# The tail of a fused attention and tree feed-forward kernel: other order of the last batch's gathers, one value sum moved to TensorE, one tree moved behind the last gather's issue

## The reference

```python
x = x + xattn(layernorm(x), ctx_1024, ctx_1024, ...)   # 16 heads of 64, 2048 keys
x = x + attn(layernorm(x), ...)                        # 8 heads of 16: xpos, decay mask, group norm, silu gate
x = x + ffn(layernorm(x), ...)
...
def _fff(x, nw, nb, w1, b1, w2, b2, act):              # a tree: 8 levels, 256 leaves
    node = jnp.zeros(x.shape[:2], dtype=jnp.int32)
    for _ in range(DEPTH):
        logit = jnp.einsum('bsd,bsd->bs', x, nw[node]) + nb[node]
        node = 2 * node + 1 + (logit > 0).astype(jnp.int32)
    leaf = node - NN
    h = act(jnp.einsum('bsd,bsdl->bsl', x, w1[leaf]) + b1[leaf])
    return jnp.einsum('bsl,bsld->bsd', h, w2[leaf]) + b2[leaf]
...
    q, k, v = _fff(xn, *q_params, relu), _fff(xn, *k_params, relu), _fff(xn, *v_params, relu)
    att = softmax(einsum('bqd,bkd->bqk', q, k) / sqrt(D))
    y = xn + einsum('bqk,bkd->bqd', att, v)
    return y + _fff(y, *f_params, gelu)
```

## Time and profile before

| | us |
|---|---|
| median of 3 executions | 669.51 |
| lowest, highest | 668.91, 670.25 |
| the profiled execution | 669.95 |
| its span (first to last instruction) | 667.8 |
| PE busy | 622.6 (93% of the span) |
| DVE busy | 452.3 (68%) |
| ACT busy | 394.2 (59%) |
| POOL busy | 275.8 (41%) |

### The profile page before, as it was taken

How to read it: one execution, slowest core, us unless ns; L and a number is a source line. 1 busy time by engine, 2 the same in 40 slices (tenths; PEclk the granted TensorE clock), 3 DMA queues, 4 the chain that set the end, 5 groups by cost and what they waited for, 6 DMA issues and landing times.

```text
span 667.8 us, 10976 instructions
## 1 busy us (share of the span) xinstructions
PE 622.6 (93%) x4225; PEld 536.9 (80%) x4225; DVE 452.3 (68%) x800; ACT 394.2 (59%) x836; POOL 275.8 (41%) x266
## 2 busy tenths in 40 slices
PE   7899999999999999898999999999999998878686
PEld 3688888999998989787988898778989897755564
DVE  2566656778776777777777777786777776853833
ACT  4665556677654555768565854957566755631541
POOL 3210002031110106896252447876161539864832
PEclk9999999999999999999999999999999999998998
DMA  9800000020100008040030037210210044203813
GB/s 197 229 33 1 1 1 0 1 64 32 33 1 1 1 2 306 19 131 0 1 132 1 1 116 276 72 60 1 80 52 1 6 157 168 68 1 128 342 61 130
DMA packets 21402, 48.54 MB, mean 73 GB/s; under 512 B 1508, under 2 KB 14696, under 8 KB 17256
## 3 DMA queue, kind: packets, MB, share of 16 engines
q0 software_dynamic: 4608, 34.74, 13.9%
q1 hardware_dynamic: 16168, 12.85, 7.1%
q10 hardware_dynamic: 576, 0.26, 0.2%
HBM read 47.59 MB, written 0.26 MB: 72 GB/s over the span
## 4 chain that ended last, share of the span: by engine, by line
PE 64%; POOL 13%; DVE 10%; ACT 6%; DMA 4%; issue 2%; SPq 1%; POOLq 0%; DVEq 0%; ACTq 0%
PE ps_s L434 22%; PE ps_av L434 20%; PE ps_ring L664 13%; PE ps_ring L434 4%; POOL leaf L1435 4%; PE ps_m L434 4%; ACT prob L993 2%; POOL leaf L1439 2%; DVE chunk_max L1286 2%; DVE pt_lo L1078 2%; DMA leaf<-up_v_dram,idx 2%; ACT pt_hi L924 2%; DMA leaf<-w_o_dram 2%; POOL ct_lo L1404 1%; DVE hid L1135 1%
## 5 line engine op out<-in xcount | busy, mean ns | idle before, releaser
L924 ACT CAST pt_hi<-ps_ring 128x512 fp32r<-128x512 f32 x256 | 144.5, 590 | 147.8 <-PE ps_ring L664 147.5
L1078 DVE TENSOR_TENSOR pt_lo<-ps_ring,pt_hi 128x512 fp32r<-128x512 f32 x256 | 170.3, 686 | 64.0 <-ACT pt_hi L924 63.9
L993 ACT ACTIVATE prob<-ps_s,neg_max 128x1024 f32<-128x1024 f32 x128 | 141.6, 1113 | 27.2 <-DVE neg_max L1369 27.1
L664 PE MATMUL ps_ring<-ident,prob 128*128 128x128 f32 x1024 | 145.0, 274 | 12.1 <-DVE q_lo L1078 4.9
L1286 DVE TENSOR_REDUCE chunk_max<-ps_s 128x1 f32<-128x1024 f32 x128 | 150.5, 1215 | 5.3 <-PE ps_s L434 5.1
L434 PE MATMUL ps_av<-pt_hi,c_hi 128*128 128x256 f32 x512 | 151.2, 295 | 0.0
L664 PEld LDWEIGHTS ps_ring<-ident,prob 128*128 128x128 f32 x1024 | 116.9, 141 | 39.3 <-issue 18.9
L434 PE MATMUL ps_av<-pt_lo,c_hi 128*128 128x256 f32 x512 | 144.7, 283 | 0.0
L434 PE MATMUL ps_av<-pt_hi,c_lo 128*128 128x256 f32 x512 | 144.7, 283 | 0.0
L434 PE MATMUL ps_s<-ct_hi,q_hi 128*128 128x512 f32 x256 | 112.5, 440 | 3.9 <-ACT prob L993 1.8
L434 PE MATMUL ps_s<-ct_hi,q_lo 128*128 128x512 f32 x256 | 101.4, 396 | 0.0
(11 more groups left out here) (267 smaller groups left out, 765.3 us busy)
## 6 DMA issues: line engine op xcount, KB each, us to landing
stage<-ctx_t_dram SPq DMA_DIRECT2D x16, 256.0 KB, 3.4
stage<-ctx_rows_dram SPq DMA_DIRECT2D x16, 256.0 KB, 2.9
leaf<-w_v_dram SPq DMA_DIRECT2D x1, 512.0 KB, 8.0
leaf<-w_o_dram SPq DMA_DIRECT2D x1, 512.0 KB, 10.2
dec<-decay_dram SPq DMA_DIRECT2D x1, 512.0 KB
nw<-node_w_dram SPq DMA_DIRECT2D x1, 510.0 KB
wsm<-w_small_dram SPq DMA_DIRECT2D x1, 448.0 KB
leaf<-wq_t_dram SPq DMA_DIRECT2D x1, 384.0 KB, 11.6
```

Source lines behind the costliest of these rows:

```text
L664: last = nc.tensor.transpose(o[:, i * P:(i + 1) * P], prob[:, n % 2, k:k + P], ident[:])
L924: nc.scalar.copy(pt_hi[:, pp, row:row + KPC, P * (n % 2):P * (n % 2 + 1)], ps_ring[:, i % 2, :].rearrange("p (k q) -> p k q", k=KPC)).then ...
L993: nc.scalar.activation(prob[:, n % 2, 1024 * e:1024 * (e + 1)], ps_s[:, 1024 * e:1024 * (e + 1)], ACT.Exp, bias=neg_max[:, n:n + 1], accum ...
L1078: return nc.vector.tensor_tensor(o, a, b_, op)
```

## The change

At the start: `w_v` and `w_o` get a semaphore each; `turn0` is issued behind the query product of slot 0 and waits for `w_v` alone, `join0` for `w_o`; ACT copies these products one slot later than before, in the middle of the slot. Third batch: POOL's `fold2` and `out2` go; PE adds the value tree's blocks instead (`value_sum`, 9 products in the place `v_half` and 8 in `v_rest`), ACT copies the sum out; the fillers of 5 and 8 there go; `y`, `y_t`, `logits_f`, `path_f` and their partners move behind the last batch's `score1` and `yv`; `res` moves behind `gate`. Its fourth tree (`hid3`, `gelu`, `down3`, `own3`, `third_sum`, `third_copy`) moves from ahead of the last batch's first trees to behind the last batch's `pick_f`. Last batch: one cast for three indices after all three picks, then gathers as up q, down q, up k, down k, up v, down v; DVE makes all of the first tree's up-product (POOL's 7 blocks go to it); the filler of 38 becomes 3, with 5 more behind the bias product. `y` and `res` of the last batch get their own room.

```diff
 BEFORE_LAST_AT = {
+    ("PE", "qk_t"): 72, ("PE", "att"): 73.5, ("PE", "v_half"): 73, ("PE", "v_rest"): 76, ("PE", "attp_t"): 76, ("PE", "attv"): 77.5, ("PE", "y_t"): 80,
+    ("PE", "logits_f"): 81, ("PE", "path_f"): 82,
+    ("ACT", "qk_t"): 73, ("ACT", "att"): 76, ("ACT", "attp_t"): 77, ("ACT", "v_sum_copy"): 78, ("ACT", "y_t"): 81, ("ACT", "gelu"): 106,
+    ("ACT", "down3"): 107,
+    ("DVE", "attmax"): 75, ("DVE", "y"): 80, ("DVE", "turns_f"): 82, ("DVE", "pick_f"): 83, ("DVE", "hid3"): 107,
+    ("Pool", "res"): 82, ("Pool", "gather3"): 83, ("Pool", "up3"): 1000, ("Pool", "weigh3"): 1000, ("Pool", "fold3"): 1000,
...
-    ("PE", "third_sum"): 90,
+    ("PE", "third_sum"): 107,
...
-    ("ACT", "load_exp"): 93,
-    ("ACT", "third_copy"): 94,
+    ("ACT", "load_exp"): 1000,
+    ("ACT", "third_copy"): 108,
...
-    ("Pool", "fold2"): 74,
-    ("Pool", "out2"): 74,
+    ("Pool", "fold2"): 1000,
+    ("Pool", "out2"): 1000,
...
-WARM = {("att", B - 2): 5, ("attv", B - 2): 8, ("gated_t", B - 1): 11, ("xf_t", B - 1): 12}
-WARM_THIRD, WARM_LAST = 18, 38
+WARM = {("gated_t", B - 1): 11, ("xf_t", B - 1): 12}
+WARM_THIRD, WARM_LAST, WARM_BLOCKS = 18, 3, 5
...
-        return (7, 10, 0) if t < 3 else (8, 8, 4)
+        return ((0, 10, 0), (7, 10, 0), (7, 10, 0), (8, 8, 4))[t]
...
-VALUE_ACT = VALUE_PE | {0: [], 1: ["turn0", "join0", "turn1"]}
+VALUE_ACT = {1: ["turn0"], 2: ["join0", "turn1"], 3: ["join1", "turn2"], 4: ["join2"], 5: ["queries"], 7: ["turn3"], 9: ["join3"]}
...
+            def value_sum(by_pool):
+
+                rows, o = down_rows_at(B - 2, 2), ps_av[:, 2 * P:3 * P]
+                if by_pool:
+                    pe.wait_ge(S["av_taken"], PAIRS)
+                    pe.wait_ge(S["got_down2"], 16 * (B - 1))
+                    mm(o, ident[:], rows[:, W1:DOWN_ROW], True, False)
+                    pe.wait_ge(S["v_weighed"], 1)
+                    for l in range(LW // 2, LW):
+                        mm(o, ident[:], rows[:, D * l:D * (l + 1)], False, False)
+                else:
+                    pe.wait_ge(S["weighed"], 4 * (B - 2) + 3)
+                    for l in range(LW // 2):
+                        last = mm(o, ident[:], rows[:, D * l:D * (l + 1)], False, l == LW // 2 - 1)
+                    last.then_inc(S["v_summed"], 1)
+
...
                     pe.wait_ge(S[f"got_down{t}"], 16 * B)
                     add(rows[:, W1:DOWN_ROW], t < 3)
+                    if t == 3:
+                        warm(WARM_BLOCKS)
                     by_act(0, n // 2)
...
-                        pe.wait_ge(S["ld_wvo"], 32)
+                        pe.wait_ge(S["ld_wv"], 16)
...
+                elif k == "v_sum_copy":
+                    act.wait_ge(S["v_summed"], 1)
+                    nc.scalar.copy(tree[:, 2, :], ps_av[:, 2 * P:3 * P]).then_inc(S["v_out_ready"], 1)
...
+                elif k == "gather_up01" and last:
+                    pool.wait_ge(S["picked"], 4 * b + 3)
+                    nc.gpsimd.tensor_copy(idx[:, 0:3], chosen[:, 0:3]).then_inc(S["idx_ready"], 3)
+                    pool.wait_ge(S["idx_ready"], 4 * b + 3)
+                    pool.wait_ge(S["ring_filled"], RING[("T", HEADS - 1, CH - 1)] + 1)
+                    pool.wait_ge(S["ring_free"], BY_DVE[("X", HEADS + 3, 0)])
+                    for t in range(3):
+                        gather_up(b, t)
+                        gather_down(b, t)
...
                 elif k == "res":
                     pool.wait_ge(S["y_ready"], b + 1)
-                    if last:
-                        pool.wait_ge(S["third_sum"], 1)
-                    nc.gpsimd.tensor_tensor(res[:], y[:], x2[:], ALU.add).then_inc(S["res_ready"], 1)
+                    nc.gpsimd.tensor_tensor(res[b], ys[b], x2[:], ALU.add).then_inc(S["res_ready"], 1)
```

More of the change, by code:

```diff
@@ L1570, in rest @@
                 elif k == "gather_up2":
[L1572 to L1573 removed]
                     if not last:
[L1576 removed]
+                        gather(b, 2)
+                elif k == "gather_down2" and not last:
+                    pool.wait_ge(S["hid_ready"], 4 * b + 2)
                     gather_down(b, 2)
```

79 lines of the change are left out of this document (37 added, 42 removed).

## The result

| | before | changed |
|---|---|---|
| median, first set (20 executions each) | 669.82 us | 671.88 us |
| lowest, highest | 666.60, 674.48 | 669.86, 675.67 |
| ratio of the first set, 95% interval | | 1.0042 (1.0027 to 1.0058) |
| ratio of a second set (6 against 23 executions) | | 1.0073 (1.0045 to 1.0101) |
| profiled execution, its span | 669.95, 667.8 | 671.89, 670.1 |

The change made the kernel slower, by 2 to 5 us (0.4% and 0.7% in the ratios). The time of 671.9 lies above the predicted range (665.4 to 670.6).

The account below looks back on a forecast made before the run. TensorE held 64% of the chain, nearly all in the 64-head pipeline; only its start and the time behind its end could move. Terms -0.45-2.5+0.4+0.1+2.0-1.4 = -1.85 gave 667.7 us, range 665.4 to 670.6.

Parts of the forecast that it names:

- Start: Start of the head pipeline: the third exponential begins when its maximum is ready, -0.45 us, bounds 0 and 0.6.
- Third batch's value sum: Behind the drain: GpSimd's fold leaves the chain for 17 TensorE products, -2.5 us, bounds 1.7 to 3.8.
- The forecast that the clock would fall again in this stretch: Drain to gate: clock low for somewhat over half of the filler of 11, limiting the gain to 2.5 us.
- Gather order: Last batch's gathers: one cast waits for the third pick, up v lands later, +0.4 us, bounds -0.2 and +0.7.
- The 0.9 us that an undisturbed queue was to give back: Last batch's gathers: without GpSimd's slow second cast, up v may land up to 0.9 us earlier.
- The condition that I had written down for a wrong prediction: Block sums: prediction wrong if `sum1` ends more than 1 us later than before, relative to up v's landing.
- Fourth tree taken out of the wait: Wait for the last batch's gathers: removal frees nothing, TensorE starts `sum0` cold, mostly hidden, +0.1 us.
- The same tree behind the last pick: Behind the last pick: GpSimd's cast ends with VectorE's product, delaying both f gathers and all behind, +2.0 us.
- The rival that the cast isn't held up: Last pick: GpSimd's cast escapes the delay, so 2.0 us leaves the sum, 665.7 us; chance 0.13.
- if the delay doesn't come, that cover still holds: Behind the last pick: the rest of the third batch's tree stays hidden even without the cast's 2.0 us delay.
- Last sum: End of the kernel: products leading up to the last sum make it 4.1 us instead of 5.48, -1.4 us.
- The slower one (671.3): Rival: cold TensorE in the block sums behind the gathers or in the last sum, 671.3 us; chance 0.13.

Follow-up runs that it names:

- cast first: Changed kernel with VectorE's product of the third batch's fourth tree waiting for GpSimd's last index cast; 673.05 us, ratio 1.0054 against the kernel before.

## Why the prediction was wrong, step by step

*Start: right and too small to matter* (-0.44 for -0.45). What I had not reckoned with is that the landing of the load ahead of it moves by 2.5 us from run to run, and that a long wait there is followed by a low clock.

*Third batch's value sum: right in kind, somewhat too large.* Taken between traces at the same clock it is -1.84, at the lower end of my bounds (1.7 to 3.8). The -3.76 between the two profiled executions is 1.84 and a fall of the clock in the trace of before that the changed one happened not to have. The forecast that the clock would fall again in this stretch holds for 11 of 14 traces with the sum on TensorE, but not for the changed kernel's profiled one. The mistake in the step: I took a fall of the clock in one trace for a property of the kernel's place when it comes in some executions and not in others. (With the fold the clock fell in one trace of three, so the two other traces of that code are 1.9 us shorter than the one I worked from.)

*Gather order: the step that failed.* I costed the order by the time at which up v lands, +0.4, and that part came out as +1.08 - 0.02: the cast began 0.76 later behind the first pick, where 0.67 was forecast, and there was 0.59 of idle time behind the cast of three columns where it was 0.28 behind one. The 0.9 us that an undisturbed queue was to give back did not come; the 17.4 us from first issue to up v's product stayed 17.4. The real loss was elsewhere, in a stretch that the sum has at +0.1. A moved DMA has to be followed into every queue in which something waits for it. I followed the order to VectorE (the first tree's product and reduction, over 5 us after the first landing, costs nothing: right) and not to GpSimd, where `up1` stands ahead of `weigh0` and waits for up k, now third. That is +2.98 between the two profiled executions, larger than any term of my sum, and with it in place of the +0.1 the forecast 667.7 would have been 670.6. About half of it is the wait itself and half the clock at which the products behind it ran; against both traces of the old code, and up to the last cast, it is 2.1 to 2.8. The condition that I had written down for a wrong prediction, that `sum1` ends over 1 us later relative to up v's landing, is what came (+2.98).

*Fourth tree taken out of the wait: right in that it costs nothing by itself.* TensorE was idle and cold as I wrote: 11.64 us idle ahead of the first product of `sum0`, clock 0.50 up to about 635. The slow spell was longer than the five or six blocks that I took, but with the weights late its price can't be told from that of the wait. The run with fillers shows that warming it ahead of the wait brings nothing as long as the weights are late. With the weights on time the stretch to the copy is 2.91 to 4.76 in six traces, five of them at half clock in the first sum (in the one with 2.91 up v came 1.1 us later), against 3.55 and 4.70 in the two traces of the old code.

*The same tree behind the last pick: right, to the hundredth* (+2.00 for +2.0, cast 2.19). One remark behind it was wrong and one holds only at full clock. The rival that the cast isn't held up, priced at a gain of 2.0, does not exist in that form: cast first, the gather's issue is held up by as much. And "if the delay doesn't come, that cover still holds" is true of the five traces without the delay in which the third batch's sum ran at full clock with 18 fillers (9.99 to 10.20 us from issue to `gelu`, 10.01 with the delay). In the one in which it ran at half clock it is what the end waits for (5.47 us, 10.96).

*Last sum: right* (-1.15 for -1.4), at a clock of 1.00.

*The rivals.* None of them happened as written. The slower one (671.3) is nearest in the time, and partly by luck: it had the right place, the block sums behind the gathers, and a low clock there is about half of the loss. But it priced the last sum at half clock, which ran at 1.00, and it had no late operand. With the weights on time a low clock in `sum0` costs little (31.0 to 32.1 us from the first issue to the last cast, against 30.9 and 31.4 with the old code), since it has time to run slowly; behind the wait it has none.

Together, at equal clock in the drain and with an equal landing at the start: -0.44 - 1.84 + 1.08 + 2.98 + 2.00 - 1.15 and -0.07 for the other stretches up to the last sum's copy are +2.6 us; the two sets gave +2.8 and +4.9 (1.0042 and 1.0073 of 669.8 and 669.4). The second set had three of its six executions at the lowest mean clock, 0.972; what made it so is not shown.

## What to carry to other kernels

When DMAs are reordered, write down for every engine queue which instruction waits for which landing, and look for work that is ready but stands behind such a wait; the engine that issues the DMAs is the first to check. Before moving a VectorE operation with two SBUF inputs next to GpSimd work, casts and gather issues alike, put one operand into PSUM or find another place. And a stretch's time from one trace has to be read with its granted clock: compare it with a second execution of the same code before a fall of the clock is booked as a cost or a gain of the edit.

## What the runs showed of the hardware that I had not expected

- A gather's issue on GpSimd takes 1.00 us alone and 2.99 beside a VectorE product of 128x2048 with two SBUF inputs; 0.99 beside the same product with one input in PSUM. A down rows' gather, 0.94 to 0.95 alone, took 2.95 beside such a product. The product itself takes 2.28 to 2.29 in all of them.
- The time of one execution goes with its mean granted clock: of the changed kernel's 20 executions the ten with a mean clock of 0.982 averaged 671.1 us, the five with 0.972 to 0.975 averaged 674.9, out of a scatter of 5.8 us from lowest to highest.
- The clock falls at the same places of the program (between 28 and 36 us, behind the wait for the load; between the drain and the gate; in the last wait), for a longer or shorter time or not at all. The same code between drain and first pick took 24.96 us without a fall, 26.3 to 26.7 with a short one and 27.7 to 27.9 with a long one; the 557.1 to 557.7 us of the heads behind the third exponential became 558.5 to 559.4 where the clock in 28 to 36 stayed low for longer.
